# First expert layer: a second top-k round ahead of the steps, Newton roots on VectorE, the second half's norm spread over steps

## The reference, cut to what matters

```python
x = x + tanh(g_xattn[0]) * L0_xattn(ctx, layernorm(x))   # sparse adjacency: sim >= its 76th largest value of the row
x = x + tanh(g_ffn[0])   * L0_ffn(layernorm(x))          # 8 experts of 176, top 2, and a shared expert of 352
x = x + tanh(g_xattn[1]) * L1_xattn(layernorm(x), ctx)   # 16 heads
x = x + tanh(g_ffn[1])   * L1_ffn(layernorm(x))          # 16 experts of 128, top 2, and a shared expert

layernorm(x) = (x - mean) / sqrt(var + 1e-5)
A = sigmoid(sim) * (sim >= threshold);  A = (A + A.T) / 2
out = (1 - gamma) * h_norm + gamma * A
```

## Time and profile before

| | us |
|---|---|
| median of three runs | 597.77 |
| the profiled execution | 597.82 |
| its span, first to last instruction | 595.1 |
| PE busy | 524.3 (88%) |
| DVE busy | 415.7 (70%) |
| ACT busy | 292.3 (49%) |
| POOL busy | 156.9 (26%) |
| mean granted TensorE clock | 0.946 |
| chain that ended last: PE / DVE / ACT | 69% / 14% / 7% |

### The profile page before, as it was taken

How to read it: one execution, slowest core, us unless ns; L and a number is a source line. 1 busy time by engine, 2 the same in 40 slices (tenths; PEclk the granted TensorE clock), 3 DMA queues, 4 the chain that set the end, 5 groups by cost and what they waited for, 6 DMA issues and landing times.

```text
span 595.1 us, 8974 instructions
## 1 busy us (share of the span) xinstructions
PE 524.3 (88%) x2762; PEld 381.4 (64%) x2762; DVE 415.7 (70%) x1101; ACT 292.3 (49%) x752; POOL 156.9 (26%) x153
## 2 busy tenths in 40 slices
PE   6787999998989988999999999999998976399970
PEld 3664788776768855666666666667665644278850
DVE  5998679974665686868686877868776876833324
ACT  3744744454564533646555454637364733045540
POOL 1032467644454602000000000101000005626660
PEclk9969999998989999999999999999999888579995
DMA  7669322321413186232140415140004601234416
GB/s 251 218 217 326 121 80 80 98 64 57 131 53 101 41 275 203 98 110 94 51 147 9 164 35 167 35 167 0 0 2 174 268 1 62 85 105 127 138 45 211
DMA packets 41875, 68.62 MB, mean 115 GB/s; under 512 B 4387, under 2 KB 31981, under 8 KB 41584
## 3 DMA queue, kind: packets, MB, share of 16 engines
q1 hardware_dynamic: 39584, 63.99, 32.2%
q0 software_dynamic: 2256, 4.20, 2.2%
HBM read 40.65 MB, written 29.49 MB: 118 GB/s over the span
## 4 chain that ended last, share of the span: by engine, by line
PE 69%; DVE 14%; ACT 7%; issue 4%; DMA 4%; POOL 2%; SPq 0%; DVEq 0%; POOLq 0%; ACTq 0%
PE bank L1356 10%; PE bank L1374 10%; PE bank L749 8%; PE bank L1407 5%; PE bank L1397 5%; PE bank L936 5%; PE bank L1418 5%; PE bank L774 3%; PE bank L1388 3%; PE bank L952 2%; PE bank L1389 2%; PE bank L1257 2%; DVE hid L710 2%; PE bank L1266 2%; POOL xn_slots L886 2%
## 5 line engine op out<-in xcount | busy, mean ns | idle before, releaser
L1561 ACT ACTIVATE silu<-bank,negm 128x256 f32<-128x256 f32 x128 | 59.7, 475 | 32.4 <-DVE negm L1798 32.2
L1569 ACT ACTIVATE probsT<-bank 128x512 f32<-128x512 f32 x64 | 38.4, 600 | 66.5 <-PE bank L1397 66.5
L1231 POOL TENSOR_TENSOR att_w_l<-att_w_raw,att_w_h 128x384 fp32r<-128x384 f32 x16 | 16.2, 1018 | 181.8 <-ACT att_w_h L1585 181.8
L1374 PE MATMUL bank<-qr,att_w_raw 128*64 128x512 f32 (+1 forms) x192 | 61.9, 605 | 2.5 <-DVE qr L1784 1.3
L671 POOL TENSOR_TENSOR ffn_w_l<-ffn_raw,ffn_w_h 128x512 fp32r<-128x512 f32 x30 | 39.0, 1301 | 56.9 <-ACT ffn_w_h L683 56.9
L695 ACT ACTIVATE hid_h<-hid 128x512 fp32r<-128x512 f32 x30 | 19.0, 633 | 62.7 <-DVE hid L710 43.0
L1798 DVE TENSOR_REDUCE negm<-bank 128x2 f32<-128x512 f32 x64 | 43.8, 686 | 6.6 <-PE bank L1389 5.6
L1806 DVE TENSOR_SCALAR hid<-silu,rden 128x256 f32<-128x256 f32 x128 | 45.2, 395 | 2.3
L1397 PEld LDWEIGHTS bank<-ident,hid 128*128 128x128 f32 x256 | 29.3, 142 | 26.6 <-issue 19.2
L1812 DVE SCALAR_TENSOR_TENSOR x<-bank,tg,x 128x512 f32<-128x512 f32 x32 | 23.8, 744 | 30.1 <-PE bank L1418 30.1
L1397 PE MATMUL bank<-ident,hid 128*128 128x128 f32 x256 | 40.9, 283 | 4.5 <-ACT probsT L1569 2.1
(11 more groups left out here) (223 smaller groups left out, 1274.6 us busy)
## 6 DMA issues: line engine op xcount, KB each, us to landing
xn_slots<-blank SPq DMA_DIRECT2D x8, 2048.0 KB, 8.5
ffn_raw<-in_w_ffn SPq DMA_DIRECT2D x30, 256.0 KB, 2.6
pair_w<-in_pair_w SPq DMA_DIRECT2D x8, 768.0 KB, 5.4
moe_w<-in_w_moe SPq DMA_DIRECT2D x1, 6144.0 KB, 18.2
folds<-att_w_raw SPq DMA_DIRECT2D x6, 896.0 KB, 7.1
att_w_raw<-folds SPq DMA_DIRECT2D x12, 384.0 KB, 3.3
moe_x<-xn_slots SPq DMA_DIRECT2D x31, 128.0 KB
ffn_raw<-in_w_ffn SPq DMA_DIRECT2D x30, 128.0 KB, 2.2
```

The source lines that it names most:

```text
L1374: last = nc.tensor.matmul(bank[2][cols, :], g_of(w_raw[b], 2 * j + w)[:, cols], qr[n % JT][:, w, :], start=(first and w == 0), stop=(not f ...
L1561: last = nc.scalar.activation(ex[u % 2][:, h, :], bank[4 + u % 2][:, h * S:(h + 1) * S], ACT.Exp, bias=negm[:, u % 2, h:h + 1], accum_out= ...
```

## The change

- `find_eight` and `take_eight` are done for two rounds ahead of the steps; body c then does round c+2, and the threshold moves from hook 9 to hook 8, the transposed adjacency on PE from 10 to 9.
- `update_second_half` is cut in two, hooks 9 and 10, each with its part of the statistics. For the second half's norm of this layer and for `n_att[0]`, the inverse root is made on DVE: a first value from the bits of the variance (two integer operations), then two Newton steps of three operations each (`invert`), then the refining step as before (`refine`) and the normalisation (`apply`). The two ACT roots at steps 11 and 17 fall away. The second half's norm has `invert` in hook 10 and the other two in hook 11; `n_att[0]` has them in hooks 17, 18 and 19.
- PE transposes `xn` ahead of the products of step 13 (before: between the products), and at the turn `pe_down` stays behind the products as in the other steps. `act_high`, `low` and the logits' copy follow in hooks 12 and 13; `add_sum` of the first half moves behind the router's shift, hook 14.
- `AHEAD` is 2.
- The attention's first weights are split in hooks 20 and 22 on ACT (before 18 and 24) and in single parts on POOL.

```diff
@@ class Norm
+                self.by_bits, self.roots = roots is None, roots
...
-            def stats(self, seq):
+            def stats(self, seq, g=None):
                 seq.wait()
-                for t in range(4 * self.hf, 4 * self.hf + 4):
+                first = 4 * self.hf
+                for t in range(first, first + 4) if g is None else (first + 2 * g, first + 2 * g + 1):
                     seq.did(nc.vector.bn_stats(bn[:, t, :], x[:, t, :]))
+                if g == 0:
+                    return
...
             def scale(self, dve, seq):
+                self.invert(dve, seq)
+                self.refine(seq)
+                self.apply(seq)
+
+            def invert(self, dve, seq):
 
                 r, w, v = rstd[:, self.tiles], root[:, self.tiles], var[:, self.tiles]
-                dve.wait_ge(self.root, self.i + 1)
-                seq.link(nc.vector.reciprocal(r, w))
+                if self.by_bits:
+                    dve.wait_ge(self.var, self.i + 1)
+                    seq.link(nc.vector.tensor_scalar(w.bitcast(I32), v.bitcast(I32), 1, None, ALU.logical_shift_right))
+                    seq.link(nc.vector.tensor_scalar(r.bitcast(I32), w.bitcast(I32), -1.0, float(0x5F3759DF), ALU.mult,
+                                                     ALU.add))
+                    self.newton(seq)
+                    self.newton(seq)
+                else:
+                    dve.wait_ge(self.root, self.roots)
+                    seq.link(nc.vector.reciprocal(r, w))
+
+            def newton(self, seq):
+                r, w, v = rstd[:, self.tiles], root[:, self.tiles], var[:, self.tiles]
+                seq.link(nc.vector.tensor_tensor(w, r, r, ALU.mult))
+                seq.link(nc.vector.scalar_tensor_tensor(out=w, in0=w, scalar=-0.5, in1=v, op0=ALU.mult, op1=ALU.mult))
+                seq.link(nc.vector.scalar_tensor_tensor(out=r, in0=w, scalar=1.5, in1=r, op0=ALU.add, op1=ALU.mult))
...
-        n_ffn0 = [Norm(later_norm, hf, hf, ((5, 6), (6, 7))[hf]) for hf in range(2)]
-        n_att = [Norm(later_norm, 2 + hf, hf, (6, 7)) for hf in range(2)]
+        n_ffn0 = [Norm(later_norm, hf, hf, ((5, 6), (6, 7))[hf], (1, None)[hf]) for hf in range(2)]
+        n_att = [Norm(later_norm, 2 + hf, hf, (6, 7), (None, 2)[hf]) for hf in range(2)]
@@ class Ffn, prog_pe
-                    turn = not st.loop and st.c == self.n - 1
-                    if turn:
-                        self.pe_down(pe, st)
+                    if not st.loop and st.c == self.n - 1:
                         before_turn()
                     self.gateup(pe, st.plus(1))
...
-                    if not turn:
-                        self.pe_down(pe, st)
+                    self.pe_down(pe, st)
@@ gpsimd
-                ffn0.prog_pool(pool, {N0 + 4: lambda: first_low_parts(0), 2 * N0 - 4: lambda: first_low_parts(1)})
+                ffn0.prog_pool(pool, {N0 + 6: lambda: low_part(0, 0, 0), N0 + 7: lambda: low_part(0, 0, 1),
+                                      2 * N0 - 5: lambda: low_part(1, 1, 0), 2 * N0 - 4: lambda: low_part(1, 1, 1)})
@@ tensor
-                                  N0 - 4: transposed_second_half,
+                                  N0 - 5: transposed_second_half,
+                                  N0 - 2: lambda: n_ffn0[1].pe_transpose(pe),
...
-                             {0: first_comb, N0 - 2: lambda: n_ffn0[1].pe_transpose(pe),
+                             {0: first_comb, 
@@ scalar
-                                    N0 - 3: lambda: n_ffn0[1].act_root(act),                                     N0 - 1: norm_second_half,
+                                    N0 - 2: lambda: n_ffn0[1].act_high(act), N0 - 1: lambda: route[0][1].act_logits(act),
                                     N0: lambda: route0_act(route[0][1], act),
-                                    N0 + 3: lambda: n_att[0].act_root(act), N0 + 4: lambda: first_high_parts(0),
+                                    N0 + 6: lambda: first_high_parts(0),
                                     2 * N0 - 5: lambda: n_att[0].act_high(act),
-                                    2 * N0 - 4: lambda: first_high_parts(1)},
+                                    2 * N0 - 6: lambda: first_high_parts(1)},
@@ vector
-                    if part == 1 and st.c < rounds - 1:
-                        find_eight(st.k + 1)
-                        if st.loop or st.c < rounds - 2:
-                            take_eight(st.k + 1)
+                    r = st.c + AHEAD
+                    if part == 1 and r < rounds:
+                        find_eight(r)
+                        if r < rounds - 1:
+                            take_eight(r)
...
+                def update_second_half(g):
+                    update(2 + g, 6 + g)
+                    dve.wait_ge(s_upd, 3 + g)
+                    n_ffn0[1].stats(seq, g)
+
+                    if g:
+                        n_ffn0[1].invert(dve, seq)
+
+                def sum_first_half():
+                    route0_shift(route[0][1], dve, seq)
                     ffn0.add_sum(dve, 0)
...
-                find_eight(0)
-                take_eight(0)
+                for r in range(AHEAD):
+                    find_eight(r)
+                    take_eight(r)
...
-                                    N0 - 5: threshold_second_half, N0 - 4: update_second_half,
-                                    N0 - 3: lambda: n_ffn0[1].scale(dve, seq), N0 - 1: low_second_half,
-                                    N0: lambda: route0_shift(route[0][1], dve, seq), N0 + 1: lambda: route0_choose(route[0][1], dve, seq),
-                                    N0 + 2: second_rows, N0 + 3: lambda: n_att[0].scale(dve, seq),
+                                    N0 - 6: threshold_second_half,
+                                    N0 - 5: lambda: update_second_half(0), N0 - 4: lambda: update_second_half(1),
+                                    N0 - 3: refine_second_half, N0 - 2: lambda: n_ffn0[1].low(dve), N0: sum_first_half, N0 + 1: lambda: route0_choose(route[0][1], dve, seq),
+                                    N0 + 2: second_rows, N0 + 3: lambda: n_att[0].invert(dve, seq), N0 + 4: lambda: n_att[0].refine(seq),
+                                    N0 + 5: lambda: n_att[0].apply(seq),
```

More of the change, by code:

```diff
@@ L302, in act_root @@
             def act_root(self, act):
+                assert not self.by_bits
                 act.wait_ge(self.var, self.i + 1)
@@ L306, in scale, with refine @@
             def scale(self, dve, seq):
+                self.invert(dve, seq)
+                self.refine(seq)
+                self.apply(seq)
+            def invert(self, dve, seq):
                 r, w, v = rstd[:, self.tiles], root[:, self.tiles], var[:, self.tiles]
-                dve.wait_ge(self.root, self.i + 1)
-                seq.link(nc.vector.reciprocal(r, w))
+                if self.by_bits:
[13 more added lines that the diff above has]
+                seq.link(nc.vector.scalar_tensor_tensor(out=r, in0=w, scalar=1.5, in1=r, op0=ALU.add, op1=ALU.mult))
+            def refine(self, seq):
+                r, w, v = rstd[:, self.tiles], root[:, self.tiles], var[:, self.tiles]
                 seq.link(nc.vector.tensor_tensor(w, r, r, ALU.mult))
@@ L313, in scale, with apply @@
                 seq.link(nc.vector.tensor_scalar(w, w, -0.5, 1.5, ALU.mult, ALU.add))
-                seq.link(nc.vector.tensor_tensor(r, r, w, ALU.mult))
+                seq.did(nc.vector.tensor_tensor(r, r, w, ALU.mult))
+            def apply(self, seq):
+                seq.wait()
                 for t in range(4 * self.hf, 4 * self.hf + 4):
@@ L353, in build @@
         first_norm, later_norm = sems("l0_att_norm", *norm_steps[0:3]) + [None] * 3, sems("norm", *norm_steps)
-        n_l0att = [Norm(first_norm, hf, hf, None) for hf in range(2)]
-        n_ffn0 = [Norm(later_norm, hf, hf, ((5, 6), (6, 7))[hf]) for hf in range(2)]
-        n_att = [Norm(later_norm, 2 + hf, hf, (6, 7)) for hf in range(2)]
-        n_ffn1 = [Norm(later_norm, 4 + hf, hf, (0, 1) if hf == 0 else (6, 7)) for hf in range(2)]
+        n_l0att = [Norm(first_norm, hf, hf, None, hf + 1) for hf in range(2)]
+        n_ffn0 = [Norm(later_norm, hf, hf, ((5, 6), (6, 7))[hf], (1, None)[hf]) for hf in range(2)]
+        n_att = [Norm(later_norm, 2 + hf, hf, (6, 7), (None, 2)[hf]) for hf in range(2)]
+        n_ffn1 = [Norm(later_norm, 4 + hf, hf, (0, 1) if hf == 0 else (6, 7), 3 + hf) for hf in range(2)]
         route_sems = [sems("l0_route", "logitsT_done", "logitsT_ready", "logits_done", "activated", "shifted", "comb_ready", "comb_transposed",
@@ L1054, in build @@
         s_top, s_rep = sems("topk", "eight_found", "eight_taken")
+        AHEAD = 2
         kth, rounds = (TOPK - 1) % 8, (TOPK + 7) // 8
@@ L1755, in threshold_second_half, with refine_second_half @@
                     threshold(3)
-                def update_second_half():
-                    update(2, 6)
-                    update(3, 7)
```

(9 more changed lines are left out.)

8 lines of the change are left out of this document (1 added, 7 removed).

## The result

The changed kernel takes 588.48 us (median of 4 runs, 587.63 to 588.81) against 597.09 us of the kernel before beside it: ratio 0.9886, 95% interval 0.9839 to 0.9932, so 1.1% faster. The forecast was 595.5, and the time lies at the lowest edge of its range (588.5). The profiled execution took 587.63 us, span 585.8, mean granted clock 0.960 (before 597.82, 595.1, 0.946).

What follows compares the result with a forecast made beforehand. PE bounds undisturbed expert steps (4.24 us), DVE the top-k steps (4.55). Gains 2.4 + 0.8 plus 0.3, partly counted already, made 3.3; less a 1.5 us clock fall, plus 0.5: 597.8 - 2.3 = 595.5 us, range 588.5 to 599.5.

Steps and rivals of the forecast that it cites:

- The turn as the largest gain: At steps 12 to 14, down products get products ahead to hide behind, ending waits of 1.29 and 1.80 us; largest gain.
- The threshold gives nothing, the adjacency waits 1.1 us: At step 10, the earlier threshold gains nothing: PE waits 1.1 us for the adjacency, against 0.96 one step later today.
- The meetings with POOL: At both norms, DVE's short operations and normalisations run into POOL's subtractions; a 128x4 operation takes 1.27 us against 0.17.
- Rival 1: DVE's short operations slip in front of POOL's at both norms: 11.3 us less, 586.5; half missed, 591. Chance 0.22.
- its floors: Without meetings: 26.6 us from 111.70 to step 15's products, 27.7 with the adjacency's wait; then 36.8 to step 23; run 586.5.
- Their price: Cost of the POOL meetings: losses 1.85 and 2.2 us at the first place; 1.9, 1.2, 1.6 and 0.45 at the second.
- The slack of 1.3 us: Lateness a steady step bears: `hid_h` ends at 189.06, the down product reading it starts at 190.33.
- I charge one fall to the new kernel: One stretch at half clock behind PE's waits in the expert steps, about 1.5 us, taking the gain to 1.8.
- gave 0.5 back: Allowance of 0.5 us for normalisations that overlap with POOL better than one by one.
- the clock follows the new waits: Waits of 1.2 to 2.5 us at steps 11, 12, 18, 19, 20 drop the clock, 1.5 us each; up to 602. Chance 0.10.
- ScalarE's table loads: In both norms, the loads for root and back to silu, 1.28 us each, go; silu and weight split lose 2.5 us lateness.
- What counts is DVE's chain: Removing the roots' table loads is to be counted on DVE's chain up to the next `hidden`, not on ScalarE.

Runs made afterwards that it cites:

- turn_only: Kernel before with only PE's new order at the turn (transposes, logits and products ahead of the downs, add_sum later): 593.31 us, ratio 0.9949; steps 1 to 23 112.82 us.
- pool_short: Changed kernel with GpSimd subtracting only an eighth of the columns in steps 8 to 11 and 17 to 19 (stale numbers left): 584.94 us, ratio 0.9793.
- beside_att: Changed kernel with the attention norm's pieces right behind `hidden`, ahead of `hid_l`, and its normalisations in two pairs: 587.83 us, ratio 0.9837.
- before_again: The kernel before, unchanged, run once more: 597.01 us, ratio 1.0026.
- round_only: Kernel before with only the second top-k round done ahead of the steps: 593.83 us, ratio 0.9952; steps 1 to 15 72.45 us.
- round_again: Second run of the kernel before with only the second top-k round ahead of the steps: 594.22 us, ratio 0.9980; steps 1 to 15 73.57 us.
- att_only: Kernel before with only the attention norm's Newton steps in three hooks and the attention weights' split moved: 593.08 us, ratio 0.9971.
- act_roots: Changed kernel with both inverse roots back on ScalarE, table loads included: 592.34 us, ratio 0.9931; steps 1 to 23 112.66 us.
- act_apply: Changed kernel with the attention norm's pieces ahead of `hid_l` and the second half's four FFN normalisations on ScalarE: 588.32 us, ratio 0.9894.

## Why the prediction was right or wrong

- **The turn as the largest gain:** right, and shown by turn_only alone. The downs of steps 12 and 13 no longer wait. From step 1 to the products of step 15 it takes 72.51 us, where 143 less 70.31 makes 72.7; to step 23 it takes 40.24 more, where some 41 were forecast.
- **The threshold gives nothing, the adjacency waits 1.1 us:** right (0.95).
- **The meetings with POOL:** right in kind, shown by pool_short and beside_att; the forms predicted are there (0.67 to 1.27 us for short operations, 3.81 and 2.80 for four normalisations). The Trainium skill (SBUF — State Buffer, Who interferes with whom) says that a Vector instruction with two SBUF inputs, or in a two-port mode, and a GpSimd instruction that reads SBUF shut each other out. These traces agree, with 1.22 and 0.17 us for the same operation with and without POOL's long one. Rival 1, the meetings missed, did not occur; near its floors came pool_short (36.8 forecast, 36.38 measured; for steps 1 to 15, 41.39 us to the products of step 10 and the floor of 26.6 without the adjacency's wait make 68.0 forecast, 68.17 measured).
- **Their price:** mis-sized. Prediction: 1.1 + 1.85 + 2.2 at the first place, 4.7 + 0.45 at the second, 10.3 us. Measured against pool_short: 4.34 and 3.86, 8.2 us. The single waits were 1.27 for 1.85, 1.09 for 2.2, and 1.45, 0.54, 0.96 for 1.9, 1.2, 1.6. The gain in the steps, at full clock, was 4.31 us for 3.3. The slack of 1.3 us was a misreading too: it takes the end of `hid_h` from the timeline and the start of the down product from the chain's rows, which lie 0.16 us later (190.33 for 190.17, 187.53 for 187.37); by the timeline it is 1.1.
- **"I charge one fall to the new kernel":** the step that failed. None came in three traces. The sum took 1.5 us off the gain for it and gave 0.5 back, which left 2.3; measured in the steps is 4.31, and the 2.0 between them are 1.5 - 0.5 + 1.0, the last for the price above. The prediction knew that the clock falls twice in the kernel before (0.87 and 0.90 in the earlier trace rows), but not that losing these falls would be the larger part of the gain, about 2.4 us. The rival "the clock follows the new waits" counted places, five of them, at 1.5 us each. Counted over the traces, the clock fell behind the single wait of 2.5 us, or already in its last microsecond, in 5 of 5 (before, before_again, round_only, round_again, turn_only); behind 1.28 and 1.80 in succession in 4 of 5 (not in round_only); behind 1.45 us or less with a step between them in none of 5 (the second place of the changed kernel, its two repeats, att_only and act_roots); and not behind 1.73 and 0.49 (turn_only) or 2.02 and 0.50 (act_roots), one trace each. Whether the length of a wait alone decides, no run shows. A fall cost 1.1 to 1.5 us over the same instructions (7.60 and 7.98 us against 6.49), and att_only keeps PE busy 0.92 us less without one; the 1.5 that I took was at the upper end.
- **ScalarE's table loads:** gone as forecast, and worth nothing net (act_roots). "What counts is DVE's chain" was right; that the chain costs as much on DVE as over ScalarE, I did not weigh.
- **The rest of the measured difference:** of the 9.3 us between the two spans, 5.0 lie outside the steps. The 2.4 ahead of step 1 can't be put down to the change (its start moved by 5.6 us between two runs of one kernel). Over its three comparisons the change is worth 0.6 to 1.1%, and the recorded 588.48 is the lowest median of them; that it came down to the edge of the range is in part luck of what lies outside the steps. The forecast of 0.4% was too small in each, by the two terms above, though within the interval of the third (0.9911 to 0.9973). The prediction also held that a time under 591.8 needs rival 1. Two of the three medians lie under it (588.48 and 591.56), and rival 1 occurred in none.

## What to carry to other kernels

Compare PE's busy time and the granted clock over the same instructions before you price an order. Where the time is longer and the clock lower than in an undisturbed stretch, the wait ahead of it has cost clock too. Cutting one long wait into several short ones can then pay even when the idle time stays the same; here it gave 0.76 us (att_only, one trace). Short operations on VectorE are cheap only while GpSimd isn't streaming, so put them ahead of what releases GpSimd (3.0 us here, beside_att), or give them to ScalarE (0.6 us, act_apply). Moving a root off ScalarE is worth what it takes off the path, not the table loads that it removes.

## What the runs showed of the hardware

- Whether the granted clock falls behind the same waits isn't fixed: round_only 1.00, round_again 0.77 and 0.66 in the 3 us windows, waits the same within 0.01 us.
- Four 128x256 normalisations: 1.40 to 1.49 us on VectorE with GpSimd short, 2.80 to 3.81 beside its subtractions, 2.07 on ScalarE beside them.
- Seven waits of PE, 6.26 us by their brackets, went with 8.20 us of the way; part of the difference are short stalls without a bracket (0.26 us at down 11 for `hid_l`).
- The meeting holds GpSimd too: in beside_att, beside VectorE's moved operations, one of its 128x512 subtractions took 1.74 us and one 1.62, where 1.29 is usual.
